# Queries and keys projected for two heads on half the array's rows each, and heavy rows fetched and stored by indirect DMA

## What is computed

```
light:  xn = rmsnorm(x);  q, k, v = xn Wq, xn Wk, xn Wv   (8 heads of 64, windows of 128 rows)
        out = softmax(q k^T / 8) v Wo                      (2 windows an image)
route:  s = x . token; 50 iterations of  a = log k - logsumexp(s + b); b = -relu(s + a)
        the 128 rows with the highest score ask, all 256 rows are context, weighted by score
heavy:  q from the 128 chosen rows, k and v from the 256 rows, 8 heads of 64,
        softmax, v, Wo, times the score, put back on the chosen rows
```

## Time and profile before

| | us |
|---|---|
| runs | 546.28, 550.07, 549.18; median 549.18 |
| profiled execution | 545.69 |
| its span, first to last instruction | 543.8 |
| busy in the span: PE, PE weight loads | 494.1, 428.1 |
| DVE, ACT, POOL | 394.1, 403.2, 229.5 |

### The profile page before, as it was taken

One profiled execution on the slowest core, in us unless ns is written; L12 is line 12 of the kernel. 1 busy time (PEld: TensorE's weight loads), 2 busy tenths in 40 slices (PEclk: granted clock), 3 DMA queues, 4 the chain that ended last, 5 costly groups with the idle time before them and its releaser, 6 DMA issues.

```text
span 543.8 us, 12420 instructions
## 1 busy us (share of the span) xinstructions
PE 494.1 (91%) x3955; PEld 428.1 (79%) x3955; DVE 394.1 (72%) x1328; ACT 403.2 (74%) x1512; POOL 229.5 (42%) x281
## 2 busy tenths in 40 slices
PE   3588878658999999999999799999999999999996
PEld 1477666546888888888888677899999999899995
DVE  6558999967888888888887883665566666666652
ACT  2278999766999999999998586676666656666662
POOL 6326667753333344333442233434334334443343
PEclk9999999988999999999999899999999999999999
DMA  8830000001000000000000000000000000010001
GB/s 237 305 147 11 28 24 30 30 20 39 3 0 2 1 2 2 1 2 1 2 2 1 1 1 12 11 11 21 20 21 21 20 20 20 22 31 30 11 11 31
DMA packets 15840, 16.44 MB, mean 30 GB/s; under 512 B 1728, under 2 KB 14800, under 8 KB 15520
## 3 DMA queue, kind: packets, MB, share of 16 engines
q1 hardware_dynamic: 14592, 13.93, 8.0%
q0 software_dynamic: 432, 1.31, 0.8%
q10 hardware_dynamic: 752, 0.40, 0.3%
HBM read 11.41 MB, written 4.23 MB: 29 GB/s over the span
## 4 chain that ended last, share of the span: by engine, by line
PE 70%; DVE 6%; issue 2%; ACT 2%; POOL 1%; POOLq 0%; DVEq 0%; ACTq 0%
PE bank L671 13%; PE bank L673 10%; PE bank L672 10%; PE bank L925 6%; PE bank L854 6%; PE bank L973 5%; PE bank L872 5%; PE bank L957 5%; PE bank L839 4%; PE bank L990 2%; PE bank L904 1%; ACT pr L589 1%; PE bank L999 1%; DVE left L1300 1%; DVE nmx L1269 1%
## 5 line engine op out<-in xcount | busy, mean ns | idle before, releaser
L425 POOL TENSOR_TENSOR pr<-pr,rinv 128x512 f32<-128x512 f32 x64 | 66.7, 1042 | 133.0 <-DVE rinv L1275 133.0
L440 POOL TENSOR_TENSOR pr<-pr,rinv 128x512 f32<-128x512 f32 x64 | 66.7, 1042 | 120.0 <-DVE rinv L1391 119.8
L589 ACT ACTIVATE pr<-bank,nmx 128x128 f32<-128x128 f32 x256 | 89.7, 364 | 4.7 <-DVE nmx L1269 4.6
L641 ACT ACTIVATE pr<-bank,nmx 128x256 f32<-128x256 f32 x128 | 59.6, 473 | 25.7 <-DVE nmx L1385 25.5
L1269 DVE TENSOR_REDUCE nmx<-bank 128x4 f32<-128x512 f32 x64 | 43.6, 681 | 26.8 <-PE bank L673 25.1
L589 ACT ACTIVATION_READ_ACCUMULATOR pr<-bank,nmx 128x1 f32 x256 | 52.4, 205 | 0.0
L1385 DVE TENSOR_REDUCE nmx<-bank 128x2 f32<-128x512 f32 x64 | 43.8, 685 | 8.6 <-PE bank L673 8.5
L839 PE MATMUL bank<-ident,pr 128*128 128x128 f32 x256 | 39.1, 276 | 4.3 <-POOL pr L425 4.3
L925 PE MATMUL bank<-xq,T_w 128*128 128x128 f32 x256 | 40.9, 282 | 0.4 <-ACT xq L618 0.4
L658 ACT ACTIVATE pt<-bank 128x512 f32<-128x512 f32 x64 | 38.2, 597 | 0.5 <-PE bank L957 0.4
L957 PE MATMUL bank<-ident,pr 128*128 128x128 f32 x256 | 38.5, 273 | 0.0
(11 more groups left out here) (241 smaller groups left out, 1549.5 us busy)
## 6 DMA issues: line engine op xcount, KB each, us to landing
mod_bc<-mod_rows_scratch SPq DMA_DIRECT2D x1, 3072.0 KB, 11.8
X<-in_L_attn_x SPq DMA_DIRECT2D x4, 512.0 KB, 8.9
xh_scratch<-xhs SPq DMA_DIRECT2D x16, 128.0 KB, 1.7
xh<-xh_scratch SPq DMA_DIRECT2D x16, 128.0 KB, 2.2
out<-ob SPq DMA_DIRECT2D x16, 128.0 KB, 1.8
mod_bc<-mod_rows_scratch SPq DMA_DIRECT2D x1, 1024.0 KB, 4.9
wkv_raw<-in_L_ffn_wkv_light SPq DMA_DIRECT2D x1, 512.0 KB, 10.5
wmod_sb<-in_L_wmod ACTq DMA_DIRECT2D x1, 384.0 KB, 5.2
```

Source lines behind the costliest of these rows:

```text
L425: pool.tensor_tensor(q, q, rinv[k % 4][:, :, None].broadcast_to([P, 4, P]), ALU.mult)\
L440: pool.tensor_tensor(q, q, rinv[k % 4][:, 0:2, None].broadcast_to([P, 2, N]), ALU.mult)\
L589: act.activation(pr[k % 4][:, i * P:(i + 1) * P], ps[2 + k % 2][:, i * P:(i + 1) * P], ACT.Exp, bias=nmx[k % 4][:, i:i + 1], accum_out=sum ...
```

## The change

- Light: the weights of queries and keys are only scaled and split (`split`). `project` forms, for an image, all queries (units j = 0, 1) and all keys (j = 2, 3), transposed, two heads to 128 partitions. They are evacuated once, in float32 (`project_evac`: even j on ACT, odd j on DVE), into `QT` and `KT`. `scores` runs at every second step for a whole window: eight float32 products of 64 rows, two heads in turn on rows 0 to 63 and 64 to 127 of the array, even heads into bank 2 and odd heads into bank 3.
- Heavy: the keys are projected like the values (`project_kv`), the queries by four float32 matmuls (`project_q`), scores as in the light phase, for four heads at once.
- The chosen rows are fetched by an indirect DMA of POOL from the normalised rows in DRAM, transposed by PE, and their results added to rows of `out` in DRAM by another. The round of the selection also asks for the places (`max_index`). SP stores an image when its light result is added, in the light phase.
- The lists of stages and their lags are changed.

The waits `lt["Sp"]`, `lt["p"]` and the others count units; `at_least` waits for a semaphore to reach a value.

On PE, the light phase (`scores`; `project` instead of the waits for `lt["lo"]`) and then the heavy phase:

```diff
             def scores(p, k):
-                g, b, j, par = 8 * p + k, 2 * p + k // 4, k % 4, b_par(k)
...
-                at_least(pe, lt["p"], 4 * (g - 1))
-                triple(ps[2 + k % 2][:, :].rearrange("p (h t) -> p h t", h=4),
-                       [t[:, b, w * P:(w + 1) * P] for t in (XT_hi, XT_lo)],
-                       [u[:, 4 * half:4 * half + 4, w * P:(w + 1) * P] for u in U[par]]).then_inc(lt["Sp"], 1)
+                if k % 2:
+                    return
...
+                at_least(pe, lt["p"], 8 * window)
+                for c in range(4):
+                    for i in range(2):
+                        rows = slice(i * DH, (i + 1) * DH)
+                        mm = pe.matmul(ps[2 + i][:, c * P:(c + 1) * P], QT[par][rows, c, t], KT[par][rows, c, t],
+                                       start=True, stop=True)
+                mm.then_inc(lt["Sp"], 1)
...
             def project(p, k):
...
+                if j == 0:
+                    at_least(pe, lt["qkd"], 2 * b)
+                elif j == 1:
                     at_least(pe, lt["v"], 2 * b)
...
                 else:
-                    at_least(pe, lt["lo"], 4 * b + (0, None, 1, 3)[j])
+                    pe.wait_ge(lt["qka"], 2 * b + j - 1)
...
+            def project_kv(p, k):
+                b, j = 2 * p + k // 4, k % 4
+                if j == 0:
...
+                    at_least(pe, hv["v"], 2 * b)
+                elif j == 1:
+                    pe.wait_ge(hv["ka"], b + 1)
+                elif j == 2:
+                    pe.wait_ge(hv["kd"], b + 1)
+                else:
+                    pe.wait_ge(hv["v"], 2 * b + 1)
...
             def scores_h(p, k):
...
-                at_least(pe, hv["p"], 2 * (g - 1))
-                for i in range(2):
-                    mm = triple(ps[2 + k % 2][:, i * N:(i + 1) * N], [u[:, 2 * j + i, 0:NQ] for u in U[par]],
-                                (XT_hi[:, b, :], XT_lo[:, b, :]))
+                at_least(pe, hv["p"], 4 * (2 * b + n))
+                for m in range(2):
+                    for i in range(2):
+                        rows, c = slice(i * DH, (i + 1) * DH), 2 * n + m
+                        mm = pe.matmul(ps[2 + i][:, m * N:(m + 1) * N], QT[par][rows, c, 0:NQ], KT[par][rows, c, :],
+                                       start=True, stop=True)
```

`project_kv` uses bank 7 for all of its four steps, the first two for keys and the last two for values. The lists of PE, light and heavy:

```diff
-                       ([(3, scores), (0, project), (OUT_LAG, out_light), (5, p_transpose), (0, project_v), (6, values)],
+                       ([(0, project), (OUT_LAG, out_light), (0, project_v), (6, p_transpose), (7, values), (4, scores)],
...
-                       ([(6, values_h), (0, gather), (0, project_vh), (7, g_transpose), (4, p_transpose_h),
-                         (0, project_h), (9, out_heavy), (10, scatter), (1, scores_h)], None),
+                       ([(0, row_transpose), (0, project_kv), (0, project_q), (9, out_heavy), (6, p_transpose_h),
+                         (7, values_h), (4, scores_h)], None),
```

Of ACT:

```diff
-                       ([(7, o_evac), (1, v_evac_l), (0, u_hi), (6, pt_evac_act), (3, exps), (0, cd_act)], None),
-                       ([(0, xq_evac), (10, rt_evac), (5, pt_evac_h), (7, gt_evac), (2, exps_h), (0, t_hi)], None),
+                       ([(8, o_evac), (0, project_evac), (1, v_evac_l), (7, pt_evac_act), (5, exps), (0, cd_act)], None),
+                       ([(0, xq_evac), (0, k_evac_h), (0, q_evac_h), (6, pt_evac_h), (5, exps_h)], None),
```

Of DVE:

```diff
-                       ([(5, recip), (9, finish_light), (1, u_lo), (0, top_between), (6, pt_evac), (3, neg_max)], cd_dve),
-                       ([(7, o_evac_h), (12, finish_heavy), (1, v_evac_h), (0, one_hot), (1, t_lo), (2, neg_max_h),
-                         (3, recip_h)], None),
+                       ([(4, neg_max), (5, recip), (6, pt_evac), (9, finish_light), (0, project_evac), (0, top_between)], cd_dve),
+                       ([(4, neg_max_h), (5, recip_h), (8, o_evac_h), (10, finish_heavy), (0, k_evac_h), (0, v_evac_h)], None),
```

Of POOL, with the new fetch, which `gather` calls for the next image:

```diff
-                       ([(3, normalise_h), (11, add_heavy)], None),
+                       ([(0, gather), (5, normalise_h), (11, scatter)], None),
...
+            def gather_rows(b):
+                at_least(pool, hv["xqp"], b - 1)
+                pool.indirect_dma_start(xg[b % 2][:, :], None, xh_dram, bass.IndirectOffsetOnAxis(rows_at[:, b:b + 1], 0))\
+                    .then_inc(hv[f"xg{b % 2}"], 16)
```

More of the change, by code:

```diff
@@ L148, in adaln_routed_attention @@
         left = [sb(f"left{i}", [R, N]) for i in two]
-        top8 = [sb(f"top8{i}", [R, 8]) for i in two]
         w1m = sb("w1m", [R, N])
[L151 to L154, removed]
+        top_all = sb("top_all", [R, NQ])
+        top1m = sb("top1m", [R, NQ])
+        top_at = sb("top_at", [R, NQ], U32)
+        sel = sb("sel", [R, 4, P])
+        selT = sb("selT", [P, 4, R])
+        rows_at = sb("rows_at", [P, B], U32)
         st1 = sb("st1", [P, B, C, 6])
@@ L218, in adaln_routed_attention @@
         sb = late
-        U = [[sb(f"U{i}{s}", [P, HEADS, N], F32R) for s in ("hi", "lo")] for i in two]
+        QT = [sb(f"QT{i}", [P, 4, N]) for i in two]
+        KT = [sb(f"KT{i}", [P, 4, N]) for i in two]
         V = [sb(f"V{i}", [P, C, HID]) for i in two]
@@ L277, in b_par @@
             return k // 4
[L281 to L288, removed]
+        HEAVY_PIECES = (4, 5)
         @block.sync
@@ L905, in gather, with project_q @@
-                mm.then_inc(hv["xqp"], 1)
-            def g_transpose(p, k):
-                if k % 4:
+                at_least(pe, hv["fin"], b - 3)
+                pe.transpose(ps[1][:, D:D + NQ], xg[par][:, :], ident[:, :]).then_inc(hv["xqp"], 1)
+            def project_q(p, k):
+                if k % 4 != 2:
                     return
                 b, par = 2 * p + k // 4, b_par(k)
-                if is_unit(b, 0):
-                    pe.wait_ge(lt["fin"], 2 * B)
-                at_least(pe, hv["fin"], 2 * (b - 1))
-                for i in range(C):
-                    mm = pe.transpose(ps[1][:, P + i * P:P + (i + 1) * P], G[par][:, i, :], ident[:, :])
-                mm.then_inc(hv["gtp"], 1)
@@ new lines, in _, with weights @@
+            dve.wait_ge(bc_in, 16 * 3)
+            dve.wait_ge(g_tab, 4)
+            def weights(p, k):
+                t = 2 * p + k
+                if t == 1:
+                    dve.wait_ge(w_small, 2)
+                    split(Q_w, wq_raw[:, 0, :], gam_sc[:, 0:1], 1)
+                elif t == 2:
+                    split(K_w, wkv_raw[:, 0:HID], gam_col[:, 0:1], 2)
+                elif t == 4:
+                    dve.wait_ge(wh_in, 80)
+                    dve.tensor_scalar(QH_w[:, :], wq_raw[:, 1, :], gam_sc[:, 1:2], None, ALU.mult).then_inc(w_scaled, 1)
+                elif t - 1 in HEAVY_PIECES:
+                    n = HEAVY_PIECES.index(t - 1)
+                    dve.wait_ge(w_ps, n + 1)
+                    split((KH_w, VH_w)[n], ps[7][:, :], gam_col[:, 1:2], 3 + n)
```

419 lines of the change are left out of this document (172 added, 247 removed).

## The result

The changed kernel takes 924.49 us (median of 4 runs, 920.24 to 925.08) against 547.73 for the kernel before (4 runs, 545.52 to 550.07): a ratio of 1.686, 95% interval 1.676 to 1.696. The profiled execution took 924.84 us, its span is 923.0. The forecast was 895 with a range of 760 to 980.

A forecast was written before the change was run, and what follows sets the result against it. Loops of waits between engines, with a partly lowered clock, were to bind both phases. 545.7 before + 167 light + 165 heavy + 8 + 6 + 5 - 2 = 895 us, range 760 to 980.

The forecast's parts named there:

- 11.5 and 12.9: Light loop: lengths in us of its two kinds of window at full clock, the longer where values are evacuated too.
- 1.0 more on average for the clock: Light loop: us added a window because TensorE's clock is lowered after idle time, from a span of 0 to 1.7.
- 1.1 us a heavy window: Heavy loop: cost of the lowered clock after TensorE's idle time, from a span of 0 to 2.3.
- the forecast's own bounds, 837 and 943: Whole kernel, both loops binding: 837 us with no lowered clock, 943 with all of it lowered.
- 28.5 windows: Heavy phase: windows in the 192.5 us stage, 57 of 64 steps, each 12.0 instead of 6.2 us: 165 us.
- The lock: Heavy loop: exponentials, reciprocal, product, transposes and evacuation chained from unit to unit; 10.9 us a window, 12.0 with the clock.
- The light term (167): Light loop: 25 windows at 13.2 instead of 6.52 us, 167 us more.
- 8 + 6: Selection: 8 us for `max_index` in 16 rounds; 6 us for indirect DMAs, the first standing open before the heavy rows.
- +5 and -2: First phase to light: +5 us where first loops mix with attention; -2 for fewer DVE passes and no PE stop.
- The rival at 500 us: Both loops: engines drift apart, every wait is met early, TensorE stays the bound; 545.7 - 43 and 0 to 4; 5%.
- The second rival: Scores in both loops: the two array halves don't run together, 45 us more, 940 us; 6%.

The follow-up runs named there:

- the filler: Changed kernel with sixteen unused products of 256 columns ahead of K's or V's product in three of four heavy steps; 893.03 us, ratio 1.629.
- the best version: Changed kernel with only the steps and orders of the lists changed, in both loops; 537.36 us, ratio 0.980 to the kernel before.

## Why the prediction was right, and where it was off

**The mechanism.** The forecast said that the lists lock DVE to ACT in the light loop and chain each heavy unit to the one before, and gave 13.2 and 12.0 us a window. Measured: 13.15 and 12.11. Taking one link out of each loop, without touching any instruction's length, took 96 and 125 us away. The releasers are the ones it named, too: `cd_e` by `cd_t`, `pt` by the transposes.

**The light loop's two kinds of window.** The forecast had 11.5 and 12.9 and 1.0 more on average for the clock. The scores start at 252.38, 267.23 and 278.67 in the trace: 14.85 and 11.44 us. Their neighbours, from 240.50 and to 292.90, are 11.88 and 14.23. Against 11.5 and 12.9, the short kind is hardly longer and the long kind is by 1.3 to 2; the mean holds. That it is the clock that makes this difference was not tested in this loop.

**The clock.** 1.1 us a heavy window was forecast; the filler gave 1.4 back. The loop without it is then 10.7, forecast 10.9. The two small errors cancel, which is luck. One sign was off: TensorE was to be busy about half the time, and it was for 65% of the span. And the forecast's own bounds, 837 and 943, add up from its terms to 839 and 947; nothing hangs on it.

**Number of heavy windows: the step that was mis-sized.** The sum counted 28.5 windows, those of the stage from 351.3 us, and gave the others nothing. The lock holds for all 31.5 between the first and the last maximum: 190.0 us where the sum had 165. That is 25 of the 29.5 us by which 924.5 exceeds 895. The three windows that were left out are 18 of these 25; the other 7 come from the length of a window, 12.11 after and 6.08 before where the sum took 12.0 and 6.2. Behind the last maximum there are 5.7 us more, forecast as 0. The light term (167) was 166 (25 x 6.65).

**Selection and transition.** `max_index` takes 0.406 us and a load of 0.070, together 0.476, where 0.48 was taken:

```profile
L1261 DVE FIND_INDEX8 top_at<-top_all,left 32x8 uint32<-32x256 f32 x15 | 6.1, 406 | 0.0
...
L434 POOL DMA_INDIRECT out<-rt,rows_at x16 | 25.5, 1595 | 5.5 <-DVE rt L1359 3.1 <-issue 2.3
L412 POOL DMA_INDIRECT xg<-xh_scratch,rows_at x16 | 15.9, 995 | 2.5 <-issue 0.6
```

Between last solver step and first heavy maximum the kernel is 25.4 us longer; less one light window of the 25 (6.65), that is 18.7 against 8 + 6 forecast. The indirect DMAs take POOL 1.0 and 1.6 us, inside the 3 that its waits were said to hide, and doubling the gathers left the heavy loop alone.

**From the first phase to the light one.** +5 and -2 were forecast; measured is -1.5 up to the first solver step.

**TensorE's work.** The rival at 500 us rested on 43 us less work. In the best version, with TensorE full, the light loop saves nothing and the heavy one 14.5. Where the light saving went can be added up from the distances between the starts of PE's rows, from the first to the last solver step (24 windows, 133.2 to 289.1 us before, 127.7 to 283.6 in the best version). The scores fall from 37.2 to 26.2 us. As much comes back around them: the transposes of the probabilities rise from 19.3 to 23.9, the output products from 20.5 to 23.7, the products with `U_w`, now those of queries and keys, from 34.3 to 38.4. Part of this lies at the edges of the blocks of scores:

```profile
233.12 0.60 PE L816 MATMUL bank<-ident,pr 128*128 128x128 f32 x4
233.65 1.16 PE L803 MATMUL bank<-KT,QT 64*128 64x128 f32 x16
234.74 0.39 PE L652 MATMUL bank<-XT_hi,Q_w_lo 128*128 128x256 f32 x1
```

Four transposes take 0.35 us ahead of a product on the whole array (163.12 to 163.47 in the earlier trace rows) and 0.53 ahead of the scores. The first product behind the scores takes 0.23 (the next one starts at 234.97), where the like took 0.12 (six from 162.39 to 163.12). The earlier trace rows has the 0.53 too, ahead of `values` (165.85 to 166.38), whose operands don't fill the array either. A window had one such block before and has two now. With 0.29 at its edges a block of scores costs 1.38 us and not 1.09, against 1.55 for two units before; the forecast had a saving of 0.6 a window. PE counts as busy through these gaps. Adding up the durations of removed and added work was too kind. Why the other blocks, the output products above all, take longer isn't explained, and no run changed the edges alone.

**The second rival** (halves don't run together) fell with the block of 1.09 us. Its price, 45 us, was near what the best version loses by it (55).

**A page's rule.** The page on TensorEngine Tiling (Array Packing) of the Trainium skill, section Theoretical Speedup, gives up to twice the speed for a contraction of 64 (the forecast named another section of it). The runs agree, a little below: 1.98 / 1.09 = 1.8 in the light loop, 1.92 / 1.07 = 1.8 in the heavy one.

## What to carry to other kernels

When a change makes one instruction need what two buffers hold, read the lists of all engines as one graph and look for a cycle: an engine's last act of a step that another's next step needs, and back. Such a cycle adds up the work of all the engines in it. Here the orders cost 387 us, where the whole change was worth 11 with good ones, and they were mended by moving entries in lists. Judge new arithmetic only after re-timing the kernel around it: the same instructions took 924 us and 537. And where no engine is nearly full (here the fullest had 65%), look for alternating releasers in the waits before you shorten anything.

## What was unexpected of the hardware

- Extra products that compute nothing made the heavy loop 45 us shorter (granted clock 0.76 to 0.97, 12.11 to 10.69 us a window).
- Products on different row halves need not always alternate: with 256 columns an order of two lower, two upper kept 1.07 us (alternating 1.07, one half only 1.92). With 128 columns an order of four and four took 1.61, alternating 1.09, one half only 1.98. Whether the columns or the length of the row of like products decides isn't shown.
- The light window stayed at 6.50 us in two kernels with quite different instructions, with TensorE "busy" throughout in both; at the edges of blocks that don't fill the array 0.1 to 0.2 us go by that the busy share doesn't show (0.18 ahead of a block of scores, 0.11 behind it, 0.18 ahead of `values` in the kernel before).
